# Head attention operands kept head by head: strided writes on VectorE become strided reads on TensorE

## The chip, the cores and the metric

The kernel runs on one core of a Trainium2 chip. The metric is the device time of one execution in microseconds (us), the median of several runs. One more execution was recorded by the hardware profiler; all rows below are from it. Its span is the time from the first to the last recorded instruction.

## What is computed

The input `x` and a context are 32 batches of 256 tokens with 256 features. The reference is, shortened:

```
x = x + tanh(g_xattn) * performer(layernorm(x), ctx, ctx)      # 16 heads, causal, 64 random features
x = x + tanh(g_ffn) * ffn(layernorm(x))
ffn(x):
    h = rmsnorm(x, gamma1)
    q = (h @ Wq + bq).reshape(b, t, 16, 16)
    kv = ((h @ Wdown + bdown) @ Wup + bup).reshape(b, t, 16, 32)
    k, v = split(kv)
    att = softmax(einsum('bthd,btgd->bthg', q, k) / 4)         # heads attend to heads, token by token
    out = einsum('bthg,btgd->bthd', att, v).reshape(b, t, 256)
    x = x + (out @ Wo + bo)
    h2 = rmsnorm(x, gamma2)
    gate = softmax(h2 @ Wg + bg)                               # 8 experts
    return x + einsum('btd,edf,bte->btf', h2, We, gate)
```

The change concerns the attention of heads to heads: for each token a 16 x 16 matrix of scores between its 16 query heads and its 16 key heads, and a mix of the 16 value heads by it. All is float32. Large products are made in three passes of a split into a high and a low part; the scores and the mix are plain float32 matmuls, which the trace shows as two records each.

## The kernel before

All 32 batches go through one software pipeline. Each engine has a fixed order of named steps, a "slot", that is repeated for each batch, with steps of different batches side by side (TensorE makes the scores of batch b while it makes the expert products of batch b-2). A step ends by raising a semaphore, and others wait for that count; `at("q_t", b)` is the end of step `q_t` of batch b. The orders are written out by hand and are the same before and after.

The 256 tokens of a batch lie in two halves of 128 partitions, `qkv[p, t, 768]`. The head attention of a batch goes like this:

- VectorE adds biases (`bqq`, `bkv0`, `bkv1`) into `qkv`, then turns 32 x 32 blocks with one instruction for each of queries, keys and values (`q_t` L1385, `k_t` L1426, `v_t` L1249). Of each block of 32 tokens and 32 values (2 token halves x 16 numbers) it makes one in which the 32 tokens run along the row and the 32 values down the partitions. The results `q_t`, `k_t` and `v_t` hold 32 token positions x 16 heads (or, for `v_t`, 16 numbers of a head) a partition. In the kernel before they are laid out position by position, so a turn writes each next element 16 elements (64 bytes) further.
- ScalarE spreads `q_t` into `q_bd` (two copies, L762) and `k_t` into `k_bd` (four copies, L789), each multiplied by a column of zeros and ones, so that one matmul serves several tokens and keeps them apart. GpSimd does so with `v_t` into `v_bd` (four copies, L475). `v_bd` has a column of ones beside the 16 numbers (`v_one`, L1537, once), from which the sum of the softmax comes.
- TensorE makes the scores (`head_scores`, L1928): for each of the 32 positions n one matmul with 32 columns of `q_bd` as weights and 64 columns of `k_bd` passing through, in four column tiles in turn. VectorE takes the maximum and subtracts it (`s_max`, `s_sub`), ScalarE makes the exponential into `p_bd`, VectorE turns it (`p_t`, L1327).
- TensorE makes the mix (`head_mix`, L1937): for each position a matmul with 32 columns of `p_t` as weights and 68 columns of `v_bd` passing through. VectorE turns the result (`o_tok`, L1362), and GpSimd divides by the sums (`o_n`).

Other steps that the prediction names: `x_raw` (L1322), `c_raw` and `h_raw` (L1391), turns of VectorE with both sides packed; `z` (L1142), the sum over the experts on VectorE, whose last step `a13` releases the store of the batch on the SP queue; the load of the next `x_in` stands behind that store in the SP queue, and also waits for `x1` (`x` L424 in the trace, a GpSimd addition); the statistics of `x_in` on VectorE (`bn`, L1276) wait for that load. In VectorE's slot `v_t` comes right after `a13`, then `h2_lo0`, `h2_lo1`, `ht_lo`, `smax`, and then the statistics. The feature products of the keys on TensorE (L1872) wait for `bqq` (`qkv` L1316), since they use its bank.

Of the kernel before, what the change touches and what calls it, by code (L numbers as in the profile page):

```python
# [7 lines left out]
ALU = mybir.AluOpType  # L8
ACT = mybir.ActivationFunctionType
AX = mybir.AxisListType  # L10

P = 128
NB, L, D = 32, 256, 256
T = L // P
C = D // P
H, HD = 16, 16
# [63 lines left out]
def build(nc, x_d, ctx_d, gx_d, gf_d, rf_d, g1_d, wq_d, bq_d, wdn_d, bdn_d, wup_d, bup_d,  # L80
          wo_d, bo_d, g2_d, wg_d, bg_d, we_d, out_d):
    ctx = ExitStack()
    with ctx:
        def sb(name, shape, dt=F32):
            return ctx.enter_context(nc.sbuf_tensor(name, shape, dt))
# [16 lines left out]
        sel_tok, off_tok, sel_blk = sb("sel_tok", [P, 2]), sb("off_tok", [P, 2]), sb("sel_blk", [P, 4])  # L102
# [33 lines left out]
            stage_f = sb_early("stage_f", [P, P])  # L136

        qkv = sb("qkv", [P, T, 3 * D])
        q_t, k_t, v_t = sb("q_t", [P, 32, H]), sb("k_t", [P, 32, H]), sb("v_t", [P, 32, HD])
        q_bd, v_bd = sb("q_bd", [P, 32, T, H]), sb("v_bd", [P, 32, 4, HD + 1])  # L140
        s_max, s_sub = sb("s_max", [P, 32]), sb("s_sub", [P, 32, H])
        p_bd, p_t = sb("p_bd", [P, 32, T, H]), sb("p_t", [P, 32, 32])

# [35 lines left out]
        nt = sb("nt", [P, QUADS, L])  # L179
        den3 = sb("den3", [P, 3, T, H])  # L180
        o_x = sb("o_x", [P, T, D])
        k_bd = sb("k_bd", [P, 32, 4, H])

        ctx_in, x_load, c_load = transfer("ctx_in", CHUNK_BUFFERS), transfer("x_load", 2), transfer("c_load", 2)
        store = transfer("store", 2)
# [45 lines left out]
        def at(step, b=0):  # L231
            return signal_of[step].at(step, b)

        def up(step, b=0):
            return signal_of[step].up(step, b)
# [125 lines left out]
        def _(pool):  # L361
# [109 lines left out]
            @per_batch  # L471
            def v_bd_(b):
                pool.wait_ge(*at("v_t", b))
                for a in range(4):
                    last = pool.tensor_scalar(v_bd[:, :, a, 0:HD], v_t[:, :, :], sel_blk[:, a:a + 1], 1.0, ALU.mult, ALU.mult)  # L475
                last.then_inc(*up("v_bd", b))

            @per_batch
# [73 lines left out]
            def slot(n):  # L552
                d_v_(n - 4)
                pk2_(n - 2)
                pk3_(n - 2)
                o_n_(n - 5)
                pk0_(n - 2)
                pq0_(n - 2)
                pq1_(n - 2)
                pq2_(n - 2)  # L560
                pq3_(n - 2)
                z0_(n - 5)
                x1_(n - 3)
                r2_(n - 5)
                g_r_(n - 3)
                v1_(n - 2)
                m00_(n - 2)
                m01_(n - 2)
                yb_(n - 4)
                v_bd_(n - 4)  # L570
                q_r_(n - 1)
                k_lo_(n - 1)
                m10_(n - 2)
                m11_(n - 2)
                q_lo_(n - 1)
                pk1_(n - 1)
# [34 lines left out]
        def _(act):  # L611
# [145 lines left out]
            @per_batch  # L757
            def q_bd_(b):
                if b >= 0:
                    act.wait_ge(*at("q_t", b))  # L760
                for t in range(T):
                    act.activation(q_bd[:, :, t, :], q_t[:, :, :], ACT.Copy, scale=sel_tok[:, t:t + 1])  # L762

            @per_batch
            def eq3_(b):
# [18 lines left out]
            @per_batch  # L784
            def k_bd_(b):
                if b >= 0:
                    act.wait_ge(*at("k_t", b))
                for a in range(4):
                    act.activation(k_bd[:, :, a, :], k_t[:, :, :], ACT.Copy, scale=sel_blk[:, a:a + 1])  # L789

            @per_batch
            def x010_(b):
# [64 lines left out]
            def slot(n):  # L857
# [24 lines left out]
                eq1_(n + 4)  # L882
                h_hi_(n + 6)
                q_bd_(n + 2)
                eq3_(n + 4)
                y_(n + 2)
                sq_(n + 1)
                k_bd_(n + 2)
                x010_(n + 4)
                x000_(n + 4)  # L890
# [92 lines left out]
            eq3_(2)  # L983
            we_hi2_()
            q_bd_(0)
            k_bd_(0)
            x000_(2)
            x001_(2)
# [15 lines left out]
            ek1_(3)  # L1004
            ek3_(3)
            q_bd_(1)
            ek0_(3)
            nt1_(2)
# [5 lines left out]
            sq_(0)  # L1014
            y_(1)
            k_bd_(1)
            x000_(3)
            x001_(3)
# [115 lines left out]
        def _(dve):  # L1134
# [111 lines left out]

            @per_batch
            def v_t_(b):
                dve.transpose(v_t[:, :, :].rearrange("p n d -> p d n"), qkv[:, :, 2 * D:3 * D].rearrange("p t (d g) -> p d t g", d=HD)).then_inc(*up("v_t", b))  # L1249

            @per_batch
            def h2_lo0_(b):
# [128 lines left out]
            @per_batch  # L1381
            def q_t_(b):
                if b >= 0:
                    dve.wait_ge(*at("bqq", b))
                dve.transpose(q_t[:, :, :].rearrange("p n h -> p h n"), qkv[:, :, 0:D].rearrange("p t (h d) -> p h t d", d=HD)).then_inc(*up("q_t", b))  # L1385

            @per_batch
            def h_tr_(b):
# [34 lines left out]
            @per_batch  # L1423
            def k_t_(b):
                dve.wait_ge(*at("bkv0", b))
                dve.transpose(k_t[:, :, :].rearrange("p n g -> p g n"), qkv[:, :, D:2 * D].rearrange("p t (g d) -> p g t d", d=HD)).then_inc(*up("k_t", b))  # L1426

            @per_batch
            def a11_(b):
# [104 lines left out]
                rest(wq_lo, stage_q, wq_hi, gamma1).then_inc(*up("wq_lo"))  # L1534

            def v_one_():
                dve.tensor_copy(v_bd[:, :, :, HD], sel_blk[:, :].unsqueeze(1).to_broadcast([P, 32, 4]))  # L1537

            def wdn_lo_():
                rest(wdn_lo, stage_d, wdn_hi, gamma1).then_inc(*up("wdn_lo"))  # L1540
# [27 lines left out]
            def slot(n):  # L1568
# [10 lines left out]
                a03_(n - 1)  # L1579
                a13_(n - 1)  # L1580
                v_t_(n + 1)
                h2_lo0_(n)
                h2_lo1_(n)
# [16 lines left out]
                a1g_(n)  # L1600
                a0g_(n)
                q_t_(n + 2)
                h_tr_(n + 5)
                a10_(n)
# [77 lines left out]
            wdn_lo_()  # L1682
            bqq_(0)
            q_t_(0)
            d_lo_(0)
            h_tr_(3)
# [5 lines left out]
            den_(1)  # L1692
            o_x_(1)
            v_t_(0)
            k_t_(0)
            g_bn_(1)
# [16 lines left out]
            wg_lo_()  # L1713
            p_t_(0)
            q_t_(1)
            o_tok_(0)
            s_rec_(0)
# [7 lines left out]
            g_bn_(2)  # L1725
            y01_(3)
            v_t_(1)
            y00_(3)
            q_bn_(4)
# [117 lines left out]
        def _(pe):  # L1847
# [77 lines left out]
            def head_scores(bank):  # L1925
                for n in range(32):
                    c, m = n % 4, n // 4
                    last = pe.matmul(ps[32 * c:32 * c + 32, bank, :].rearrange("p (a m g) -> p m a g", a=4, m=8)[:, m],  # L1928
                                     q_bd[:, n, :, :].rearrange("p t h -> p (t h)"), k_bd[:, n, :, :],
                                     start=True, stop=True, tile_position=(0, 32 * c))  # L1930
                return last

            def head_mix(banks):
                width = 4 * (HD + 1)
                for n in range(32):
                    a, m = n % 4, n // 4
                    last = pe.matmul(ps[32 * a:32 * a + 32, banks[m // 4], m % 4 * width:(m % 4 + 1) * width],  # L1937
                                     p_t[:, 8 * a + m, :], v_bd[:, 8 * a + m, :, :].rearrange("p c d -> p (c d)"),
                                     start=True, stop=True, tile_position=(0, 32 * a))
                return last  # L1940

# [342 lines left out]
```

## Time and profile before

| | |
|---|---|
| time, median of 3 runs | 1117.84 us (1117.04 to 1120.37) |
| the profiled execution | 1119.66 us |
| its span | 1117.9 us |
| granted TensorE clock, mean | 0.991 of full |
| busy: TensorE matmul / VectorE | 1034.7 / 938.5 us |
| busy: ScalarE / GpSimd | 757.0 / 756.8 us |

Busy time is the time in which an engine had an instruction under way. Matmuls are pipelined, so a busy TensorE is not yet one at its peak; how near it is must be read from what it waits for. `PEld` is TensorE's weight loader, which works beside the matmuls. The first 110 us or so are start-up: loads, a pass over the whole context, splitting of the weights, and the filling of the pipeline.

### The profile page before, as it was taken

What the parts mean: (1) busy time and instruction counts of PE and PEld (TensorE: products, weight loads), DVE (VectorE), ACT (ScalarE), POOL (GpSimd) and SP (SyncE); (2) the same over time, 40 slices, a digit from 0 to 9 for tenths busy, and PEclk for the clock granted to TensorE, in tenths of its full rate; (3) what the DMA queues carried; (4) which work ended last, traced back from release to release, by engine and by line L of the source; (5) the groups of instructions that cost most, each with busy time, mean ns of one, the idle gap of its engine ahead of it and who ended that gap; (6) DMA issues with size and microseconds to landing.
All of it is one profiled execution on the core that took longest, in us unless ns stands there. A gap on an engine that the chain in (4) does not pass through costs nothing.

```text
span 1117.9 us, 31579 instructions
## 1 busy us (share of the span) xinstructions
PE 1034.7 (93%) x12867; PEld 841.2 (75%) x12867; DVE 938.5 (84%) x2173; ACT 757.0 (68%) x1563; POOL 756.8 (68%) x1111
## 2 busy tenths in 40 slices
PE   0576899999999999999999999999999999999988
PEld 0355677778888888778888787888778888888776
DVE  7578678888888988888888888888888988888886
ACT  6666767667776776777677667776776677767531
POOL 3467776677767767777777667776767777777431
PEclk9988899999999999999999999999999999999999
DMA  9410000100001001010010101000000000000000
GB/s 307 142 29 11 21 30 1 30 30 30 30 30 29 11 21 30 30 30 30 30 31 2 29 30 30 30 30 30 24 8 31 29 31 30 30 30 12 11 11 19
DMA packets 38911, 38.63 MB, mean 35 GB/s; under 512 B 3440, under 2 KB 38512, under 8 KB 38768
## 3 DMA queue, kind: packets, MB, share of 16 engines
q1 hardware_dynamic: 38384, 36.59, 10.5%
q8 instruction: 102, 1.67, 0.6%
q14 instruction: 41, 0.34, 0.1%
q0 software_dynamic: 384, 0.04, 0.0%
HBM read 28.23 MB, written 8.39 MB: 33 GB/s over the span
## 4 chain that ended last, share of the span: by engine, by line
PE 52%; DVE 24%; DMA 7%; ACT 7%; POOL 6%; issue 2%; SPq 1%; POOLq 0%; DVEq 0%; ACTq 0%
PE ps L1857 10%; PE ps L1858 7%; PE ps L1859 7%; DVE z L1142 6%; PE ps L1888 6%; PE ps L1903 5%; PE ps L1872 4%; DMA c_in<-in_ctx 4%; DMA x_in<-in_x 3%; PE ps L1937 3%; PE ps L1896 3%; POOL x L424 2%; POOL z L417 2%; DVE k_t L1426 2%; PE ps L1851 2%
## 5 line engine op out<-in xcount | busy, mean ns | idle before, releaser
L1142 DVE SCALAR_TENSOR_TENSOR z<-ps,gate,z 128x256 f32<-128x256 f32 x512 | 234.5, 470 | 17.4 <-PE ps L1859 8.9
L1857 PE MATMUL ps<-we_hi,h_hi 128*128 128x512 f32 (+2 forms) x640 | 238.8, 373 | 5.8 <-DVE s_sub L1296 1.7
L1858 PE MATMUL ps<-we_lo,h_hi 128*128 128x512 f32 (+2 forms) x640 | 223.7, 350 | 0.0
L1859 PE MATMUL ps<-we_hi,h_lo 128*128 128x512 f32 (+2 forms) x640 | 223.7, 349 | 0.0
L1857 PEld LDWEIGHTS ps<-we_hi,h_hi 128*128 128x128 f32 x640 | 120.2, 188 | 44.3 <-issue 18.5
L1888 PE MATMUL ps<-qf,kf 64*128 64x256 f32 x1024 | 137.4, 397 | 11.7 <-POOL qf L408 9.4
L1859 PEld LDWEIGHTS ps<-we_hi,h_lo 128*128 128x128 f32 x640 | 120.2, 188 | 17.2
L1858 PEld LDWEIGHTS ps<-we_lo,h_hi 128*128 128x128 f32 x640 | 120.5, 188 | 11.6
L1888 PEld LDWEIGHTS ps<-qf,kf 64*128 64x128 f32 x1024 | 95.1, 191 | 36.9 <-issue 19.1
L1903 PE MATMUL ps<-att,v 128*32 128x256 f32 (+1 forms) x2048 | 112.4, 339 | 1.2 <-DVE att L1218 0.9
L475 POOL TENSOR_SCALAR v_bd<-v_t,sel_blk 128x512 f32<-128x512 f32 x128 | 88.3, 710 | 13.2 <-DVE v_t L1249 13.2
L1903 PEld LDWEIGHTS ps<-att,v 128*32 128x32 f32 x2048 | 59.3, 112 | 34.4 <-DVE z L1142 4.7
L789 ACT ACTIVATE k_bd<-k_t,sel_blk 128x512 f32<-128x512 f32 x128 | 81.5, 708 | 4.6 <-DVE k_t L1426 4.6
L1896 PEld LDWEIGHTS ps<-qf,kf 64*128 64x128 f32 x1024 | 66.8, 189 | 5.7 <-DVE ht_lo L1265 0.5
L1896 PE MATMUL ps<-qf,kf 64*128 64x128 f32 x1024 | 68.8, 273 | 0.1
L773 ACT ACTIVATE y<-x,shift_f,r_f 128x256 f32<-128x256 f32 x64 | 35.0, 594 | 49.5 <-DVE y L1155 49.5
L397 POOL TENSOR_SCALAR qf<-qf 128x512 f32<-128x512 f32 x32 | 19.9, 621 | 62.9 <-ACT qf L745 62.6
L507 POOL TENSOR_TENSOR q_lo<-x_raw,q_hi 128x512 fp32r<-128x512 f32 x32 | 41.2, 1288 | 30.4 <-ACT q_hi L689 30.4
L415 POOL TENSOR_SCALAR z<-y,tanh_f 128x512 f32<-128x512 f32 x32 | 22.1, 692 | 52.5 <-DVE y L1155 52.5
L643 ACT ACTIVATE nt<-ps 128x512 f32<-128x512 f32 x32 | 19.1, 596 | 55.9 <-PE ps L1903 55.9
L380 POOL TENSOR_TENSOR o_n<-o_tok,s_rec 128x512 f32<-128x512 f32 x32 | 41.6, 1301 | 22.2 <-DVE s_rec L1367 21.8
L739 ACT ACTIVATE ot_hi<-ps 128x512 fp32r<-128x512 f32 x32 | 19.2, 600 | 54.5 <-PE ps L1851 54.4
(218 smaller groups left out, 3077.9 us busy)
## 6 DMA issues: line engine op xcount, KB each, us to landing
x_in<-in_x SPq DMA_DIRECT2D x32, 256.0 KB, 3.3
c_in<-in_ctx SPq DMA_DIRECT2D x32, 256.0 KB, 3.7
out<-z SPq DMA_DIRECT2D x32, 256.0 KB, 2.2
c_chunk<-in_ctx SPq DMA_DIRECT2D x14, 512.0 KB, 8.9
stage<-in_L_ffn_We SPq DMA_DIRECT2D x2, 1024.0 KB, 9.6
c_chunk<-in_ctx SPq DMA_DIRECT2D x2, 256.0 KB, 8.5
stage_u<-in_L_ffn_Wup SPq DMA_DIRECT2D x2, 128.0 KB, 5.7
stage_b<-in_L_ffn_bup SPq DMA_DIRECT2D x1, 256.0 KB, 6.1
```

Source lines behind the costliest of these rows:

```text
L380: pool.tensor_tensor(o_n[:, :, :].rearrange("p t (h d) -> p d t h", d=HD), o_tok[:, 0:HD, :, :], s_rec[:, :, :].unsqueeze(1).to_broadcast( ...
L475: last = pool.tensor_scalar(v_bd[:, :, a, 0:HD], v_t[:, :, :], sel_blk[:, a:a + 1], 1.0, ALU.mult, ALU.mult)
L507: pool.tensor_tensor(q_lo[:, :], x_raw[:, :], q_hi[:, :].bitcast(F32), ALU.subtract).then_inc(*up("q_lo", b))
L789: act.activation(k_bd[:, :, a, :], k_t[:, :, :], ACT.Copy, scale=sel_blk[:, a:a + 1])
L1142: return dve.scalar_tensor_tensor(out=z[b % 2][:, t, :], in0=ps[:, bank, offset:offset + D], scalar=gate[:, t, ex:ex + 1], in1=z[b % 2][:, ...
L1857: pe.matmul(out, a_hi(c), b_hi(c), start=(c == 0), stop=False)
L1858: pe.matmul(out, a_hi(c), b_lo(c), start=False, stop=False)
L1859: last = pe.matmul(out, a_lo(c), b_hi(c), start=False, stop=(c == C - 1))
L1872: last = pe.matmul(ps[:, BANK[f"f{of}{j}"], :], weight[own, :], src[own, :], start=(n == 0), stop=(n == 2 and not more), tile_position=(32 ...
L1888: last = pe.matmul(ps[:, banks[half], j * L:(j + 1) * L], kf[r, pr, 0:P], qf[r, pr, :], start=True, stop=True)
L1896: last = pe.matmul(ps[:, banks[half], j * P:(j + 1) * P], kf[r, pr, P:L], qf[r, pr, P:L], start=True, stop=True)
L1903: last = pe.matmul(ps[32 * j:32 * j + 32, bank, half * L + part * P:half * L + L], v1[:, part, 8 * oct + 2 * j + half, :], att[:, half, j, ...
```

## The change

The turned tiles and the spread tiles are laid out with the position last: `q_t[p, head, position]` instead of `q_t[p, position, head]`, and likewise `k_t`, `v_t`, `q_bd`, `k_bd` and `v_bd`. A turn then writes packed, and the spreads read and write packed. What is contiguous for a matmul before (all columns of one position) is taken with a step of 32 elements (128 bytes) after: the weights from `q_bd`, the passing columns from `k_bd` and `v_bd`. `p_bd`, `p_t`, `s_sub` and `o_tok` are as before. Sizes, values, counts of instructions, orders and waits are the same.

```
-        q_t, k_t, v_t = sb("q_t", [P, 32, H]), sb("k_t", [P, 32, H]), sb("v_t", [P, 32, HD])
-        q_bd, v_bd = sb("q_bd", [P, 32, T, H]), sb("v_bd", [P, 32, 4, HD + 1])
+        q_t, k_t, v_t = sb("q_t", [P, H, 32]), sb("k_t", [P, H, 32]), sb("v_t", [P, HD, 32])
+        q_bd, v_bd = sb("q_bd", [P, T, H, 32]), sb("v_bd", [P, 4, HD + 1, 32])
-        k_bd = sb("k_bd", [P, 32, 4, H])
+        k_bd = sb("k_bd", [P, 4, H, 32])
     v_bd_ (GpSimd)
-                    last = pool.tensor_scalar(v_bd[:, :, a, 0:HD], v_t[:, :, :], sel_blk[:, a:a + 1], 1.0, ALU.mult, ALU.mult)
+                    last = pool.tensor_scalar(v_bd[:, a, 0:HD, :], v_t[:, :, :], sel_blk[:, a:a + 1], 1.0, ALU.mult, ALU.mult)
     q_bd_, k_bd_ (ScalarE)
-                    act.activation(q_bd[:, :, t, :], q_t[:, :, :], ACT.Copy, scale=sel_tok[:, t:t + 1])
+                    act.activation(q_bd[:, t, :, :], q_t[:, :, :], ACT.Copy, scale=sel_tok[:, t:t + 1])
-                    act.activation(k_bd[:, :, a, :], k_t[:, :, :], ACT.Copy, scale=sel_blk[:, a:a + 1])
+                    act.activation(k_bd[:, a, :, :], k_t[:, :, :], ACT.Copy, scale=sel_blk[:, a:a + 1])
     v_t_, q_t_, k_t_ (VectorE)
-                dve.transpose(v_t[:, :, :].rearrange("p n d -> p d n"), qkv[:, :, 2 * D:3 * D].rearrange("p t (d g) -> p d t g", d=HD)).then_inc(*up("v_t", b))
+                dve.transpose(v_t[:, :, :], qkv[:, :, 2 * D:3 * D].rearrange("p t (d g) -> p d t g", d=HD)).then_inc(*up("v_t", b))
-                dve.transpose(q_t[:, :, :].rearrange("p n h -> p h n"), qkv[:, :, 0:D].rearrange("p t (h d) -> p h t d", d=HD)).then_inc(*up("q_t", b))
+                dve.transpose(q_t[:, :, :], qkv[:, :, 0:D].rearrange("p t (h d) -> p h t d", d=HD)).then_inc(*up("q_t", b))
-                dve.transpose(k_t[:, :, :].rearrange("p n g -> p g n"), qkv[:, :, D:2 * D].rearrange("p t (g d) -> p g t d", d=HD)).then_inc(*up("k_t", b))
+                dve.transpose(k_t[:, :, :], qkv[:, :, D:2 * D].rearrange("p t (g d) -> p g t d", d=HD)).then_inc(*up("k_t", b))
     v_one_ (VectorE, once)
-                dve.tensor_copy(v_bd[:, :, :, HD], sel_blk[:, :].unsqueeze(1).to_broadcast([P, 32, 4]))
+                dve.tensor_copy(v_bd[:, :, HD, :], sel_blk[:, :].unsqueeze(2).to_broadcast([P, 4, 32]))
     head_scores, head_mix (TensorE)
-                                     q_bd[:, n, :, :].rearrange("p t h -> p (t h)"), k_bd[:, n, :, :],
+                                     q_bd[:, :, :, n].rearrange("p t h -> p (t h)"), k_bd[:, :, :, n],
-                                     p_t[:, 8 * a + m, :], v_bd[:, 8 * a + m, :, :].rearrange("p c d -> p (c d)"),
+                                     p_t[:, 8 * a + m, :], v_bd[:, :, :, 8 * a + m],
```

## Rows read from the trace of the kernel before

**Rows 1.** The page: busy time of each engine, share of the span.

```profile
PE 1034.7 (93%) x12867; PEld 841.2 (75%) x12867; DVE 938.5 (84%) x2173; ACT 757.0 (68%) x1563; POOL 756.8 (68%) x1111
```

**Rows 2.** Windows of 200 us: length, busy us of each engine, clock, DMA.

```profile
600.00:800.00 200.00, 197.66 (x2457) 161.90 (x2455) 173.88 (x413) 141.97 (x299) 142.90 (x209) 1.00 0.08 26
```

**Rows 3.** The chain, 550 to 640 us: start us, us, what (two scores, one mix).

```profile
551.27 0.89 PE ps L1928 x64
...
583.16 0.89 PE ps L1928 x64
...
593.46 1.03 PE ps L1937 x64
```

**Rows 4.** Waits of TensorE and its loader, 200 to 1000 us: total us, times, longest.

```profile
PE ps L1872 <- DVE qkv L1316: 5.6, 10, 0.7
...
PEld ps L1872 <- DVE qkv L1316: 8.9, 14, 0.9
PEld ps L1857 <- ACT qf L730: 5.9, 25, 0.2
PEld ps L1903 <- DVE z L1142: 4.2, 25, 0.2
PEld ps L1937 <- DVE down L1332: 4.1, 17, 0.3
```

**Rows 5.** The chain again, 600 to 635 us, three of its pieces.

```profile
602.44 1.08 DVE k_t L1426
...
614.84 5.03 DMA c_in<-in_ctx
...
629.66 1.08 DVE q_t L1385
```

**Rows 6.** Waits of VectorE, 200 to 1000 us.

```profile
DVE bn L1276 <- DMA x_in<-in_x: 28.0, 25, 2.1
DVE bn6g L1198 <- POOL x L424: 24.2, 25, 1.1
```

**Rows 7.** Groups by line and form: VectorE's turns; busy us, mean ns, idle before.

```profile
L1426 DVE STREAM_TRANSPOSE k_t<-qkv 128x512 f32<-128x512 f32 x32 | 35.1, 1098 | 1.0
L1385 DVE STREAM_TRANSPOSE q_t<-qkv 128x512 f32<-128x512 f32 x32 | 34.2, 1070 | 0.0
L1249 DVE STREAM_TRANSPOSE v_t<-qkv 128x512 f32<-128x512 f32 x32 | 33.8, 1057 | 0.0
...
L1362 DVE STREAM_TRANSPOSE o_tok<-ps 128x544 f32<-128x544 f32 x32 | 23.6, 739 | 1.9 <-PE ps L1937 1.9
...
L1322 DVE STREAM_TRANSPOSE x_raw<-xn 128x512 f32<-128x512 f32 x32 | 22.3, 697 | 0.7 <-ACT xn L670 0.6
```

**Rows 8.** Line L1519 in the start-up: ns min/median/max of two instructions.

```profile
L1519 DVE TENSOR_TENSOR wup_lo<-stage_u,wup_hi x2: 416/710/1003, 61.8 to 62.1; 128x256 fp32r<-128x256 f32 x2
```

**Rows 9.** Timeline of VectorE: start us, us, what.

```profile
629.66 1.08 DVE L1385 STREAM_TRANSPOSE q_t<-qkv 128x512 f32<-128x512 f32 x1
630.57 0.70 DVE L1391 STREAM_TRANSPOSE h_raw<-h2e 128x512 f32<-128x512 f32 x1
631.17 0.99 DVE L1142 SCALAR_TENSOR_TENSOR z<-ps,gate,z 128x256 f32<-128x256 f32 x2
```

**Rows 10.** Groups by line and form: spreads and their nearest packed likes.

```profile
L475 POOL TENSOR_SCALAR v_bd<-v_t,sel_blk 128x512 f32<-128x512 f32 x128 | 88.3, 710 | 13.2 <-DVE v_t L1249 13.2
L789 ACT ACTIVATE k_bd<-k_t,sel_blk 128x512 f32<-128x512 f32 x128 | 81.5, 708 | 4.6 <-DVE k_t L1426 4.6
...
L805 ACT ACTIVATE h2n<-y,r 128x256 f32<-128x256 f32 x64 | 28.8, 501 | 2.8 <-POOL r L431 2.8
...
L415 POOL TENSOR_SCALAR z<-y,tanh_f 128x512 f32<-128x512 f32 x32 | 22.1, 692 | 52.5 <-DVE y L1155 52.5
```

**Rows 11.** Groups by line and form: the mix and score matmuls, 32 batches.

```profile
L1937 PE MATMUL ps<-v_bd,p_t 128*32 128x68 f32 x2048 | 36.9, 224 | 4.7 <-POOL down_v L365 2.1 <-DVE p_t L1327 1.5 <-DVE down L1332 0.6
...
L1928 PE MATMUL ps<-k_bd,q_bd 128*32 128x64 f32 x2048 | 36.2, 225 | 0.0
```

## The prediction

> **What bounds the kernel now.** I read the page first. TensorE is busy for 93% of the span, VectorE for 84%, the other two for 68% [rows 1]. The windows view says more, because it leaves the start out: between 600 and 800 us TensorE is busy 197.7 of 200 us at the full clock, VectorE 173.9 [rows 2]. The reader is to see that a batch of the steady part has almost no time in which TensorE has nothing in hand. One batch takes 31.9 us: the same stage, the 64 small score matmuls, starts at 551.27 and at 583.16 us [rows 3].
>
> The waits view of TensorE shows how close it is to its own bound. Over 25 batches (200 to 1000 us) it and its weight loader waited 5.6 + 8.9 us for the bias addition on `qkv`, 5.9 us for ScalarE's exponential, 4.2 us for the last `z` and 4.1 us for `down` [rows 4]. That is 28.7 us, or 1.15 us in each batch of 31.9. So TensorE's own work would need about 30.75 us a batch, and 1.15 us is all that a quicker VectorE or ScalarE could give it.
>
> The chain that ended last shows the second loop. It does not stay on TensorE: through the batch after 600 us it runs over VectorE's `k_t` turn, GpSimd's `z` and `x1`, the last `z` of the batch before, the store and load on SP, the `c_in` transfer (5.03 us), and back over `q_t` to the next `k_t` [rows 5]. This loop takes the same 31.9 us. Two loops of equal length hold each other: shortening one alone brings little beyond the slack that the other has, lengthening either costs.
>
> VectorE itself waits in each batch for `x_in` to land (28.0 us over 25) and for `x1` (24.2 us) [rows 6].
>
> **The three turns on VectorE.** `k_t`, `q_t` and `v_t` take 1098, 1070 and 1057 ns for 512 elements a partition. `x_raw`, the same operation and size with both sides packed, takes 697 ns [rows 7]. Two things differ: the three read runs of 16, and they write every element 64 bytes after the last. The change leaves the reads and makes the writes packed. Which one costs? `o_tok` reads with a step of 17 elements (from PSUM) and writes packed: 739 ns for 544 elements, the packed rate. And in the start-up two `wup_lo` subtractions of equal size take 416 and 1003 ns; the slower is the half whose elements are written (and `wup_hi` read) 64 bytes apart [rows 8] (GpSimd was at work beside it, so its size is not clean). I put the cost on the written step. Since neighbours on VectorE overlap a little, I take start-to-start times: `q_t` to the next 0.91 us, the packed `h_raw` to the next 0.60 us [rows 9]. Saving 0.31 us a turn, 0.93 us a batch; bounds are nothing (if the reads are to blame) and 1098 + 1070 + 1057 - 3 x 697 = 1.13 us.
>
> Not all of it counts. `v_t` stands between the last `z` of a batch, which releases the store and the next `x_in` load, and the batch statistics that wait for this `x_in`; VectorE waits there 1.1 us in every batch [rows 6], so 0.31 us saved in `v_t` becomes 0.31 us more of waiting. `q_t` and `k_t` lie on the second loop [rows 5]: 0.62 us a batch is what that loop becomes shorter.
>
> **ScalarE and GpSimd.** The spreads write the same 512 elements, from packed to packed instead of in runs of 16. `k_bd` takes 708 ns; the scaled copy `h2n` of 256 elements, packed, takes 501, and both are (708 - 501)/256 = 0.81 ns an element: no cost of the runs is to be seen, so I take nothing. The far bound is an unscaled 512-element copy at about 0.6 us, 0.1 us less for each of six. `v_bd` takes 710 ns against 692 for the packed `z` product [rows 10]: 4 x 0.018 = 0.07 us a batch. Both engines are idle for 32% of the span [rows 1], and that covers it. `v_one` runs once.
>
> **The matmuls.** Here the change adds. A batch has 64 score matmuls of 64 columns and 64 mix matmuls of 68 [rows 11]: 32 products, two records each, spread over four column tiles that run side by side. The scores take 0.89 us: 16 records follow one another in a tile, so a column takes 0.89/(16 x 64) = 0.87 ns. The mix takes 1.03 us, 0.95 ns a column [rows 3]. In this form each column comes from the address next to the last. After the change each comes 128 bytes further, in `k_bd` and `v_bd`, and so do the 32 columns of each `q_bd` weight load. No row shows TensorE reading like that. Bounds: nothing, if a stream that asks for a column every 0.87 ns gets it from anywhere. From the other side, the nearest row is VectorE's stream in steps of 64 bytes, an element in 0.91/512 = 1.78 ns [rows 9]. If TensorE's four streams each fall to that pace, a column costs 0.91 ns more in the scores and 0.83 in the mix: 16 x 64 x 0.91 = 0.93 us and 16 x 68 x 0.83 = 0.90 us, 1.83 us a batch. The outer bound is that the four streams then also take turns: 64 x 64 x 0.87 = 3.56 us instead of 0.89, 64 x 68 x 0.87 = 3.79 instead of 1.03, 5.43 us a batch. I take 1.83. It is a stream to SBUF that I compare with a stream from it, of another engine: that is the weakest link of this prediction.
>
> The Trainium skill (Advanced Engine Details and Errata, Memory Cachelines) speaks against the change at this place: SBUF has lines of 16 bytes, and a stream needs at least two hits in a line or it pays. Packed float32 has four hits a line, a step of 128 bytes has one. The page says nothing of its size or of TensorE in particular; by it the sum has some cost above nothing. The turns on VectorE agree with it, 1070 against 697 ns [rows 7]; for TensorE nothing here shows it.
>
> The strided weight loads of `q_bd` have 32 columns each; at 0.9 ns more a column a load grows by 29 ns, and it lies behind a matmul of its own tile that then takes 64 x 1.78 = 114 ns. Taken at nothing; if that cover fails, see the rivals.
>
> **The sum.** TensorE: 30.75 + 1.83 = 32.6 us of own work. The second loop: 31.9 - 0.62 = 31.3, now 1.3 us shorter than TensorE's, so most of TensorE's waits go: each is a wait for something that the added 0.9 us in front of it lets arrive. The score results are used by `s_max`, behind which VectorE waits for `x_in` anyway [rows 6], so their lateness goes no further. I let 0.25 us of the 1.15 us of waits stay: 32.85 us a batch, 0.95 more than 31.9. Times 32 batches is 30.4 us. On the profiled execution (span 1117.9, whole time 1119.66) this gives a span of 1148 and a time of 1150; the median of the runs shown is 1.8 us lower than that execution, so **1148 us**. With all waits gone it is 0.7 x 32 = 22 us (1140), with none gone 1.83 x 32 = 59 (1177). The likeliest case's own range is 1133 to 1180.
>
> **The rivals.**
> *TensorE reads the step for nothing (chance 0.25).* For it: its float32 columns come at only 0.87 ns, slowly for a stream. Then VectorE's 0.62 us a batch count, within TensorE's slack of 1.15: -0.62 x 32 = -20 us, 1098 us. It decides up to an added cost of about 0.9 us a batch (what TensorE's waits absorb), that is 0.9/2112 = 0.43 ns for each of the 16 x 132 = 2112 columns a batch: under 1.3 ns a column the kernel is not slower.
> *The four streams share one path (0.18).* Against it: today four run at 0.87 ns a column each without slowing each other. For it: a shared path may be just wide enough for packed columns. 5.43 - 0.9 = 4.53 us a batch, +145: 1263 us, and TensorE the only bound.
> *The weight loads are what grows (0.07).* The 64 loads of the scores start 13.9 ns apart; if they are made one after another and a load then takes 32 x 1.78 = 57 ns, the scores take 3.65 us, +2.76, with the 0.90 of the mix 3.66, less 0.9: 2.76 x 32 = +88, 1206 us.
> *The turns do not get faster, since the runs of 16 that they read are what costs (0.05).* Then the second loop stays 31.9, TensorE's waits go only in part: about +1.3 x 32 = 42, 1160 us.
>
> **The numbers.** The forecast has 0.45. A measurement of this kernel tells a difference of 0.3% (3.4 us) from none. Faster by more holds most of the free rival: 0.22. Within 0.3% lies the narrow strip where the added cost is near 0.9 us a batch: 0.06. Slower: 0.72. The range has to hold cases of both signs: from 1096, just below the free rival, up to 1245, which leaves out most of the shared path and little else.
>
> **What the profile after would show.** The three turns at about 0.7 us. The score stage at 1.8 us and the mix at 1.9 instead of 0.89 and 1.03 in the chain. The waits for `qkv` and `down` on TensorE nearly gone, its busy share above 99%. VectorE's wait for `x_in` in each batch no shorter. `k_bd`, `q_bd` and `v_bd` unchanged within 0.02 us. The prediction is wrong if the score stage keeps 0.9 us (then 1098) or takes over 3 us (then above 1200), or if the stages grow as said and TensorE keeps its waits.

## The result

The changed kernel takes 1187.6 us (median of 5 runs, 1185.84 to 1189.66) against 1117.5 us (median of 5 runs of the kernel before; three of them gave the 1117.84 above): the ratio is 1.062 (95% interval 1.060 to 1.064), 70 us slower. The forecast was 1148 us with a range of 1096 to 1245: the right side and inside the range, but 30 us of a loss of 70. The profiled execution took 1185.84 us, with a span of 1184.1.

### The profile after

The page, busy time of each engine and the chain by engine, answers to [rows 1]:

```profile
PE 1112.0 (94%) x12867; PEld 928.1 (78%) x12867; DVE 919.4 (78%) x2173; ACT 755.9 (64%) x1563; POOL 758.4 (64%) x1111
...
PE 87%; DVE 4%; ACT 4%; POOL 2%; DMA 1%; issue 1%; SPq 0%; DVEq 0%; POOLq 0%; ACTq 0%
```

VectorE has less to do than before, and the chain now runs over TensorE for 87% of the span; before it was 52%, with VectorE at 24%. The window of [rows 2] after the change:

```profile
600.00:800.00 200.00, 199.81 (x2375) 167.54 (x2378) 159.25 (x388) 133.05 (x281) 137.36 (x200) 1.00 0.08 25
```

TensorE is busy in 199.8 of 200 us, at the full clock as before. The groups by line and form: turns, matmuls and weight loads, to be held against [rows 7] and [rows 11].

```profile
L1928 PE MATMUL ps<-k_bd,q_bd 128*32 128x64 f32 x2048 | 90.8, 358 | 0.0
...
L1928 PEld LDWEIGHTS ps<-k_bd,q_bd 128*32 128x32 f32 x2048 | 82.8, 158 | 0.3 <-issue 0.3
...
L1937 PE MATMUL ps<-v_bd,p_t 128*32 128x68 f32 x2048 | 66.5, 295 | 3.8 <-POOL down_v L365 2.1 <-DVE p_t L1327 1.1 <-DVE down L1332 0.5
...
L1426 DVE STREAM_TRANSPOSE k_t<-qkv 128x512 f32<-128x512 f32 x32 | 22.7, 710 | 1.0
L1385 DVE STREAM_TRANSPOSE q_t<-qkv 128x512 f32<-128x512 f32 x32 | 22.4, 700 | 0.0
L1249 DVE STREAM_TRANSPOSE v_t<-qkv 128x512 f32<-128x512 f32 x32 | 22.4, 699 | 0.0
```

The turns are at 0.70 us as forecast. A mix record went from 224 to 295 ns, a score record from 225 to 358: the two stages read with the same step and do not pay the same. How long a stage is shows best from its first start to the start of the group behind it. The timeline of TensorE after, start us, us (the last end is modelled, so a group's own length is longer than the way to the next start; the 1.03 us of the mix in [rows 3] has such an end), what:

```profile
611.29 2.83 PE L1928 MATMUL ps<-k_bd,q_bd 128*32 128x64 f32 x64
613.79 0.98 PE L1903 MATMUL ps<-att,v 128*32 128x256 f32 x16
...
623.41 2.08 PE L1937 MATMUL ps<-v_bd,p_t 128*32 128x68 f32 x64
625.28 0.86 PE L1903 MATMUL ps<-att,v 128*32 128x256 f32 x16
```

The same view before:

```profile
582.98 1.08 PE L1928 MATMUL ps<-k_bd,q_bd 128*32 128x64 f32 x64
583.87 0.83 PE L1903 MATMUL ps<-att,v 128*32 128x256 f32 x16
...
593.34 1.16 PE L1937 MATMUL ps<-v_bd,p_t 128*32 128x68 f32 x64
594.28 0.86 PE L1903 MATMUL ps<-att,v 128*32 128x256 f32 x16
```

The scores went from 0.89 to 2.50 us, the mix from 0.94 to 1.87 us. The first group behind the scores also starts slower, by 0.15 us (0.91 instead of 0.76 us to the next). Together 1.61 + 0.15 + 0.93 = 2.69 us a batch on TensorE, where the forecast had 1.83.

I took such stage starts from the timelines of all batches between 200 and 1000 us and averaged the distances. One batch: 32.10 us before, 34.37 after, so 2.27 us more; TensorE gave back 2.69 - 2.27 = 0.42 us of waiting. The same starts give a check that needs no wait: the shortest batches before take 31.72 us, and 31.72 + 2.69 = 34.41 us is what a batch takes after, to 0.04 us. The waits view of the weight loader after answers to [rows 4]:

```profile
PEld ps L1857 <- ACT qf L730: 5.4, 23, 0.2
PEld ps L1903 <- DVE z L1142: 3.9, 23, 0.2
```

The waits for `qkv` and `down` are gone. Those for ScalarE and for `z` are as they were in each batch (0.2 us), although a batch is 2.3 us longer. And VectorE, against [rows 6]:

```profile
DVE s_max L1270 <- PE ps L1928: 45.4, 24, 2.0
DVE z L1142 <- PE ps L1859: 22.1, 26, 1.0
...
DVE qkv L1316 <- PE ps L1859: 18.4, 24, 0.9
...
DVE bn L1276 <- DMA x_in<-in_x: 0.5, 2, 0.3
```

It no longer waits for `x_in` (28.0 before, 0.5 after): it waits for the scores instead (45.4), right before. The prediction had expected this wait for `x_in` to stay as it was.

### The profile page after: what moved, and what is told of

Its sections match the earlier page's. It is cut to its first block, busy times and chain, and to the rows that moved or that the text cites. A ratio compares the mean times of both kernels' runs of the same rounds, so it can differ in the third digit from the quotient of the medians.

```text
span 1184.1 us, 31579 instructions
## 1 busy us (share of the span) xinstructions
PE 1112.0 (94%) x12867; PEld 928.1 (78%) x12867; DVE 919.4 (78%) x2173; ACT 755.9 (64%) x1563; POOL 758.4 (64%) x1111
## 4 chain that ended last, share of the span: by engine, by line
PE 87%; DVE 4%; ACT 4%; POOL 2%; DMA 1%; issue 1%; SPq 0%; DVEq 0%; POOLq 0%; ACTq 0%
PE ps L1857 15%; PE ps L1859 12%; PE ps L1858 12%; PE ps L1888 10%; PE ps L1903 7%; PE ps L1928 7%; PE ps L1937 5%; PE ps L1896 5%; PE ps L1872 5%; PE ps L1851 2%; PE ps L1913 2%; PE ps L1921 1%; PE ps L1922 1%; DMA c_chunk<-in_ctx 1%; ACT k_bd L789 1%
## 5 line engine op out<-in xcount | busy, mean ns | idle before, releaser
L1142 DVE SCALAR_TENSOR_TENSOR z<-ps,gate,z 128x256 f32<-128x256 f32 x512 | 235.7, 472 | 43.2 <-PE ps L1859 31.7
L1903 PEld LDWEIGHTS ps<-att,v 128*32 128x32 f32 x2048 | 69.7, 115 | 31.6 <-DVE z L1142 4.7
L1928 PE MATMUL ps<-k_bd,q_bd 128*32 128x64 f32 x2048 | 90.8, 358 | 0.0
L1928 PEld LDWEIGHTS ps<-k_bd,q_bd 128*32 128x32 f32 x2048 | 82.8, 158 | 0.3 <-issue 0.3
L1937 PE MATMUL ps<-v_bd,p_t 128*32 128x68 f32 x2048 | 66.5, 295 | 3.8 <-POOL down_v L365 2.1
L489 POOL TENSOR_TENSOR k_lo<-c_raw,k_hi 128x512 fp32r<-128x512 f32 x32 | 41.5, 1298 | 40.8 <-ACT k_hi L664 40.7
L1270 DVE TENSOR_REDUCE s_max<-ps 128x32 f32<-128x512 f32 x32 | 22.1, 692 | 57.9 <-PE ps L1928 57.9
L1937 PEld LDWEIGHTS ps<-v_bd,p_t 128*32 128x32 f32 x2048 | 58.4, 124 | 8.1 <-issue 2.9
```

The lines of the kernel that those rows point to most:

```text
L1142: return dve.scalar_tensor_tensor(out=z[b % 2][:, t, :], in0=ps[:, bank, offset:offset + D], scalar=gate[:, t, ex:ex + 1], in1=z[b % 2][:, ...
L1903: last = pe.matmul(ps[32 * j:32 * j + 32, bank, half * L + part * P:half * L + L], v1[:, part, 8 * oct + 2 * j + half, :], att[:, half, j, ...
```

## The experiments

All times are medians; those of the kernel before, run beside them, were 1117.5 (with the first four kernels below `after`), 1117.4 (steps 2 and 4, swapped positions, one tile after the other), 1119.5 (both kernels with spreads that take a step, and the other order) and 1117.7 us (the last). "Scores" and "mix" are stage lengths from start to next start, medians of the batches between 200 and 1000 us; "one batch" is the mean there.

| kernel | scores | mix | one batch | time | ratio, interval |
|---|---|---|---|---|---|
| before | 0.89 | 0.94 | 32.10 | 1117.5 | |
| after | 2.50 | 1.87 | 34.37 | 1187.6 | 1.062 (1.060 to 1.064) |
| keys and values | 2.66 | 1.87 | 34.44 | 1189.7 | 1.064 (1.061 to 1.068) |
| queries only | 1.33 | 0.94 | 32.37 | 1124.1 | 1.006 (1.004 to 1.008) |
| values only | 0.89 | 1.87 | 33.02 | 1146.1 | 1.025 (1.022 to 1.029) |
| keys only | 2.65 | 0.94 | 33.53 | 1163.4 | 1.0405 (1.037 to 1.044) |
| keys and values, positions swapped | 1.77 | 2.71 | 34.52 | 1190.9 | one run |
| keys only, one tile after the other | 5.3 | 2.9 | 38.70 | 1326.4 | one run |
| step 2 | 0.96 | 1.01 | 32.13 | 1116.7 | 0.9987 (0.9974 to 1.0000) |
| step 4 | 1.91 | 1.98 | 33.80 | 1169.4 | 1.046 (1.044 to 1.048) |
| turns packed, spreads write with a step | 0.89 | 0.94 | 33.14 | 1150.0 | 1.028 (1.025 to 1.030) |
| turns packed, spreads read with a step | 0.89 | 0.94 | 33.66 | 1169.1 | 1.045 (1.042 to 1.048) |
| after, scores issued in another order | 1.79 | 1.88 | 33.55 | 1162.4 | 1.039 (1.036 to 1.043) |
| step 2 for queries and keys only | 0.97 | 0.94 | 32.05 | 1114.7 | 0.9969 (0.9954 to 0.9985) |

The scores vary from batch to batch where they are long or their weight loads have a step: 2.50 to 2.70 us in `after`, 2.53 to 2.68 with keys and values, 1.31 to 1.39 with the queries only. Each of the two kernels whose spreads take a step has one long batch near 200 us (37.6 and 38.3 us); without it their means are 32.95 and 33.45.

### Parts of the change

Four kernels have only some of the tiles head by head. For the keys the edit is

```
-        k_bd = sb("k_bd", [P, 32, 4, H])
+        k_bd = sb("k_bd", [P, 4, H, 32])
-                    act.activation(k_bd[:, :, a, :], k_t[:, :, :], ACT.Copy, scale=sel_blk[:, a:a + 1])
+                    act.activation(k_bd[:, a, :, :], k_t[:, :, :], ACT.Copy, scale=sel_blk[:, a:a + 1])
-                dve.transpose(k_t[:, :, :].rearrange("p n g -> p g n"), ...
+                dve.transpose(k_t[:, :, :], ...
-                                     q_bd[:, n, :, :].rearrange("p t h -> p (t h)"), k_bd[:, n, :, :],
+                                     q_bd[:, n, :, :].rearrange("p t h -> p (t h)"), k_bd[:, :, :, n],
```

and the lines of the change's own diff for the queries and for the values.

Keys and values:

> Keys and values head by head as in the changed kernel, queries (q_t, q_bd) as before: the passing columns of scores and mix come with a step of 32, the weight loads are packed. Theory 1, the strided weight loads are what makes the score stage 0.8 us longer than forecast (2.50 instead of about 1.8 us): scores 1.8 us, mix 1.87 us. Rival, the score stage's passing columns alone cost that much (a score matmul writes runs of 16 in PSUM, the mix one run of 68): scores stay at 2.5 us. For the time: the changed kernel gained 70 us for 2.7 us of added TensorE time a batch, 26 us for each; if that holds here, 1.86 us gives +48, 1166 us. If TensorE's waits absorb 0.9 us a batch as the prediction had it, about 1148 us.

The timeline:

```profile
578.55 2.93 PE L1928 MATMUL ps<-k_bd,q_bd 128*32 128x64 f32 x64
581.21 0.92 PE L1903 MATMUL ps<-att,v 128*32 128x256 f32 x16
```

The scores took 2.66 us with packed weight loads, more than the 2.50 with strided ones (why more is open). Theory 1 fell: the weight loads are not what makes the scores longer than forecast. Both expected times, 1166 and 1148 us, were too low as well: 1189.7.

Queries only:

> Only the queries head by head: 64 weight loads of 32 columns a batch come with a step of 32, all passing columns are packed. Theory 1a, a strided load is slower whatever passes: 57 ns or so instead of 27, and as it does not hide behind a matmul of 56 ns the score stage grows by 0.5 to 0.8 us, to 1.4 to 1.7 us; time about 1117 + 0.8 x 26 = 1138, less what the shorter q_t gives. Theory 1b, a strided load hides behind packed columns and costs only where the passing columns are strided too: score stage 0.9 to 1.0 us, and the time 1110 to 1118, because q_t is 0.31 us shorter.

The timeline shows the strided weight loads alone:

```profile
587.17 1.58 PE L1928 MATMUL ps<-k_bd,q_bd 128*32 128x64 f32 x64
588.56 0.84 PE L1903 MATMUL ps<-att,v 128*32 128x256 f32 x16
```

1.39 us here and 1.33 as the median, 0.44 to 0.50 more: at the lower end of theory 1a. With packed columns a strided load does not hide; in the changed kernel, whose columns are slower, it adds nothing to be seen. The time rose by 6.6 us (1138 less something was expected) and a batch by 0.27 us, less than the stage.

Values only:

> Only the values head by head: mix 1.87 us instead of 0.94, scores 0.89 as before, v_t 0.70 us. If TensorE's waits of before (1.15 us a batch by the waits view) absorb up to 0.9 us, the time stays within 1115 to 1123 us. If nearly none of them is time that could be filled, +0.93 us a batch at 26 us each: 1141 us. The wait for x_in takes up what v_t saves in either case.

Keys only:

> Only the keys head by head: scores 1.8 us instead of 0.89, mix as before. Absorbing theory: the shorter k_t (0.31 us on the second loop) and the waits cover it, 1112 to 1120 us. Rival: +0.93 us a batch at 26 us each, 1141 us. Together with the values alone it should give the time of keys and values together, if TensorE is the only bound.

Here is the second error. The values add 0.93 us a batch to TensorE and a batch grows by 0.92: nothing is absorbed, and the time is 1146 instead of 1115 to 1123. The keys add about 1.8 us (the stage, 2.6 and not the 1.8 expected, and the start of the group behind) and a batch grows by 1.43: 0.4 us is absorbed. The two losses, 28.6 and 45.9 us, add up to 74.5 us, against 72.2 for keys and values together. The timeline of the kernel before tells where the slack lies. The key features behind the scores that start at 582.98 (above), and the scores and key features of the next batch:

```profile
590.54 0.50 PE L1872 MATMUL ps<-k_hi,f_hi 32*128 32x512 f32 x4
...
614.71 1.08 PE L1928 MATMUL ps<-k_bd,q_bd 128*32 128x64 f32 x64
...
623.03 0.51 PE L1872 MATMUL ps<-k_hi,f_hi 32*128 32x512 f32 x4 [0.71 <-DVE qkv L1316]
```

The distances are 7.56 and 8.32 us. Over 24 batches it is 7.84 us on average and 7.54 at least: some 0.3 us a batch is a wait that can be filled, not the 14.5/25 = 0.58 that the waits view gives. The next distance, to the mix, is 2.88 us on average against 2.81 to 2.82 with the keys, with both and after: 0.07 us. Together this is 0.4 us, not 1.15, and it is also what lies between the mean batch and the shortest one, 32.10 - 31.72. The shortest batch plus the stages' growth gives the batches of other kernels too: with the values 31.72 + 0.93 = 32.65 us (the shortest there is 32.64, the mean 33.02), with the keys 31.72 + 1.83 = 33.55 (33.48, 33.53), with a step of 4 31.72 + 2.06 = 33.78 (33.76, 33.80). With the values alone the 0.4 us stay unfilled. Both lie between the scores and the mix, so growth in the scores uses them. Growth in the mix comes behind, and VectorE waits for the mix itself. Its waits with the values alone:

```profile
DVE bn L1276 <- DMA x_in<-in_x: 30.8, 25, 2.3
...
DVE z L1142 <- PE ps L1859: 16.5, 25, 0.7
...
DVE o_tok L1362 <- PE ps L1937: 3.9, 7, 0.9
```

`z` waited 2.5 us for TensorE over the same stretch before and waits 16.5 now. I read it so: the lateness goes to the last `z`, from there to `x_in` and to the `qkv` that TensorE waits for, and its wait stays (the distance is 7.83 us on average, as before). The two loops of the prediction are then one, as VectorE's part hangs on TensorE's products. The waits fit this; no run cuts the path.

### Why the scores pay more than the mix

Both read with a step of 128 bytes. But the scores give neighbouring positions to the four column tiles that run side by side, the mix gives them positions 8 apart. The next kernel swaps this. Its products go where they went but come from other positions, so its output is not the attention; sizes and counts are the same.

```
-                                     q_bd[:, n, :, :].rearrange("p t h -> p (t h)"), k_bd[:, :, :, n],
+                                     q_bd[:, 8 * c + m, :, :].rearrange("p t h -> p (t h)"), k_bd[:, :, :, 8 * c + m],
-                                     p_t[:, 8 * a + m, :], v_bd[:, :, :, 8 * a + m],
+                                     p_t[:, n, :], v_bd[:, :, :, n],
```

> Keys and values head by head as in the run with both, but the positions are taken in the other order: the four column tiles of the scores, which run side by side, read positions 8 apart (32 bytes), those of the mix read neighbouring positions (4 bytes apart). The products are those of permuted positions. Theory: what makes a strided score column cost 2.5 ns and a strided mix column 1.7 ns is that in the scores the four tiles read at nearly the same addresses. Then the stages change places: scores 64/68 of 1.87 us, about 1.75 us, mix about 2.7 us. Rival: it is the output (the scores write runs of 16, the mix one run of 68) or the stage itself: scores stay at 2.6 us, mix at 1.87 us.

The timeline of TensorE:

```profile
579.24 1.97 PE L1928 MATMUL ps<-k_bd,q_bd 128*32 128x64 f32 x64
581.00 0.85 PE L1903 MATMUL ps<-att,v 128*32 128x256 f32 x16
...
590.47 3.09 PE L1937 MATMUL ps<-v_bd,p_t 128*32 128x68 f32 x64
593.33 0.89 PE L1903 MATMUL ps<-att,v 128*32 128x256 f32 x16
```

Scores 1.76 us, mix 2.86 us (1.77 and 2.71 as medians): the stages changed places, as the theory says, and the rival, the way in which the output is written, fell, since that did not change. The other half of the argument leaves each product where it was and changes only the order of issue in the changed kernel, so that no two of the four tiles are less than 5 positions apart (each is 9 from its neighbour in the issue, but for the wrap at 8):

```
-                for n in range(32):
+                for n in (4 * ((m + 2 * c) % 8) + c for m in range(8) for c in range(4)):
```

> The changed kernel with the 32 score products issued in another order only: the four tiles that run side by side take positions 9 or more apart instead of neighbours, each into the place in PSUM that it had. Theory (neighbouring positions read at once are what makes a strided score column cost 2.5 ns instead of 1.7): scores 1.8 to 2.0 us instead of 2.50, 0.5 to 0.7 us less a batch, all of it on TensorE: 1167 to 1173 us instead of 1187.6. If the strided weight loads then show (0.5 us in the run with the queries alone), scores 2.3 us and 1181 us. If nothing comes of the order: 1187 us.

The timeline:

```profile
599.72 1.98 PE L1928 MATMUL ps<-k_bd,q_bd 128*32 128x64 f32 x64
601.51 0.84 PE L1903 MATMUL ps<-att,v 128*32 128x256 f32 x16
```

This order also changes which places of the output are written side by side; in the swapped kernel they stayed as they were, so the reading is what both have in common. The scores take 1.79 us instead of 2.50, and the kernel 1162.4 instead of 1187.6 us: 25 us come back for one line, a little more than the 15 to 21 expected. At 1.79 us the stage pays 0.88 ns more than packed for each of the 1024 columns that pass through one tile in a batch, about the size that the prediction had for it (0.91), and the strided loads cost almost nothing beside them (1.79 us against 1.77 with packed ones).

Is the cost one of each stream or of the four together? One kernel (keys head by head) goes through the positions of one tile before the next, in both stages:

```
-                for n in range(32):
+                for n in (4 * m + c for c in range(4) for m in range(8)):
```

> Keys alone head by head; and both stages go through the eight positions of one column tile before the next tile, so that the matmuls no longer run side by side in four tiles. The mix then shows a lone packed stream, the scores a lone strided one. If a strided stream is limited by itself (each column goes to another place and takes about 1.7 ns however many tiles run), a score record takes 64 x 1.7 = 110 ns or more against 60 to 80 for a packed mix record: 64 records 7 us against 4 to 5 us. If the limit is one that the four streams share, a lone strided stream runs at the packed pace and the scores take no longer than 64/68 of the mix.

The timeline, lone strided columns in the scores, lone packed ones in the mix:

```profile
600.57 5.56 PE L1928 MATMUL ps<-k_bd,q_bd 128*32 128x64 f32 x61
...
605.96 0.40 PE L1928 MATMUL ps<-k_bd,q_bd 128*32 128x64 f32 x2
...
615.76 3.15 PE L1937 MATMUL ps<-v_bd,p_t 128*32 128x68 f32 x61
...
618.74 0.34 PE L1937 MATMUL ps<-v_bd,p_t 128*32 128x68 f32 x3
```

61 score records take 605.96 - 600.57 = 5.39 us, 88 ns each or 1.38 ns a column; 61 mix records take 2.98 us, 49 ns each or 0.72 ns a column (a weight load that does not hide would be in both). A lone stream pays for the step by itself, about twofold. With four side by side a column of a tile takes 0.87 ns packed, 1.72 with a step and 8 positions apart, and 2.4 to 2.6 with a step and neighbouring. So part of the price is each stream's own, and a second part comes only when tiles that run side by side read neighbouring addresses. The one run took 1326.4 us, since the tiles' overlap was given up.

### How long a step may be

`S` neighbouring positions stand innermost in all six tiles:

```
+        q_t, k_t, v_t = sb("q_t", [P, G, H, S]), sb("k_t", [P, G, H, S]), sb("v_t", [P, G, HD, S])
+        q_bd, v_bd = sb("q_bd", [P, G, T, H, S]), sb("v_bd", [P, G, 4, HD + 1, S])
+        k_bd = sb("k_bd", [P, G, 4, H, S])
+                                     q_bd[:, n // S, :, :, n % S].rearrange("p t h -> p (t h)"), k_bd[:, n // S, :, :, n % S],
```

with G = 32/S, and the turns, spreads and the mix to match. The step is then S elements, and a turn writes runs of S.

> All six tiles laid out with pairs of neighbouring positions innermost: the matmuls read with a step of 2 elements (8 bytes), the turns write runs of 2. By the 16-byte lines of the Trainium skill (Advanced Engine Details and Errata, Memory Cachelines) two reads still fall into one line, so that scores and mix stay at 0.9 us; a cost that comes with any step would give 1.8 and 2.5 us. The turns lie between 0.70 and 1.07 us; if runs of 2 are enough for the writes, 0.70 us, and q_t and k_t bring the second loop down by 0.6 us a batch: 1100 us. If neither changes, 1117 us.

> As the step of 2, with four neighbouring positions innermost: a step of 4 elements (16 bytes). Every column then is in a line of its own, as with the step of 32. Theory of lines: scores 2.5 us and mix 1.87 us as in the changed kernel, and its time, about 1187 us. [...] The turns write runs of 4 (16 bytes): 0.70 us.

The timelines of the scores, step 2 and then step 4 (in these kernels the lines stand one further down):

```profile
585.02 1.16 PE L1929 MATMUL ps<-k_bd,q_bd 128*32 128x64 f32 x64
585.99 0.84 PE L1904 MATMUL ps<-att,v 128*32 128x256 f32 x16
...
604.63 2.10 PE L1929 MATMUL ps<-k_bd,q_bd 128*32 128x64 f32 x64
606.54 0.85 PE L1904 MATMUL ps<-att,v 128*32 128x256 f32 x16
```

With a step of 2 the stages are 0.96 and 1.01 us, 0.07 more than packed each; with a step of 4, 1.91 and 1.98. The large price comes between 8 and 16 bytes. That is where the lines of the Trainium skill (Advanced Engine Details and Errata, Memory Cachelines) have it, two reads in a line of 16 bytes, and TensorE's times fit the rule, but for the 7 to 8% that 8 bytes cost. The distance beyond a line is not what costs: the mix takes 1.98 us at 16 bytes and 1.87 at 128. The scores with a step of 4 did not take the 2.5 us expected, though their four tiles read neighbours as well, and the time was 1169.4 us and not 1187. Neighbours cost more only at the wide step, and why is open.

The turns took 0.70 us with runs of 2 already, and yet the time did not move. The waits of VectorE with a step of 2 say why:

```profile
DVE bn L1277 <- DMA x_in<-in_x: 29.3, 25, 2.2
...
DVE z L1143 <- PE ps L1860: 10.6, 27, 0.9
...
DVE s_max L1271 <- PE ps L1929: 5.3, 24, 0.2
```

`z` waits 10.6 us for TensorE instead of 2.5 and `s_max` 5.3: some 13 us over 25 batches of the 23 that the turns gave back went into waiting for products. A batch stayed at 32.13 us and the time at 1116.7, where the second loop would have given 1100.

### The turns without TensorE's part

> The VectorE part of the change alone: the three turns write packed (head by head), and the spreads of ScalarE and GpSimd bring the numbers back into position order by writing with a step, so that every matmul reads packed as before. Turns 0.70 us, scores 0.89, mix 0.94. As the prediction had it (q_t and k_t on a second loop that is as long as TensorE's): 0.62 us a batch, 1098 us. As the run with a step of 2 suggests (the turns were 0.7 us there and nothing came of it, VectorE only waited more for TensorE): 1112 to 1118 us. If strided writes cost ScalarE and GpSimd as much as VectorE (0.3 us or more each, ten a batch), later than that: above 1121 us.

> As the run before, but the spreads read with a step and write in runs of 16. Turns, scores and mix the same. The question is only which side of a spread bears a step better: k_bd and q_bd at 0.71 and 0.72 us, v_bd at 0.70 us if a step costs these engines nothing, about 1 us and more if it costs them what it costs VectorE. Time as in the run before if both are free.

The turns write packed, TensorE reads packed, and the spreads do the reordering:

```
-                    act.activation(k_bd[:, :, a, :], k_t[:, :, :], ...
+                    act.activation(k_bd[:, :, a, :].rearrange("p n g -> p g n"), k_t[:, :, :], ...
```

(in the second kernel the `rearrange` stands on `k_t`). Groups by form, spreads writing with a step:

```profile
L475 POOL TENSOR_SCALAR v_bd<-v_t,sel_blk 128x512 f32<-128x512 f32 x128 | 144.8, 1228 | 13.8 <-DVE v_t L1249 13.8
L789 ACT ACTIVATE k_bd<-k_t,sel_blk 128x512 f32<-128x512 f32 x128 | 129.4, 1162 | 3.5 <-DVE k_t L1426 3.5
```

1.23 and 1.16 us instead of 0.71 [rows 10]; reading with a step costs as much, 1.18 and 1.19. `q_bd` takes 1.25 and 1.26 us instead of 0.72. Ten spreads a batch pay where three turns gained, and the last expectation, above 1121 us, is the one that held: 1150 and 1169 us. The waits of TensorE tell the place (spreads writing with a step):

```profile
PEld ps L1857 <- DVE z L1142: 23.7, 23, 1.1
...
PE ps L1857 <- ACT att L794: 22.7, 24, 2.8
```

ScalarE's copies of `att` stand behind the four `k_bd`, and TensorE waits for them; before, this wait came in one batch of 25 (0.9 us).

### A version that is a little faster

Queries and keys with a step of 2, values as before:

> Queries and keys with a step of 2 as in that run, values position by position as in the kernel before. v_t is 1.06 us again, the mix 0.94 us. The step of 2 cost 0.05 us a batch in the mix and gave 0.31 us in v_t; if v_t's saving is worth nothing (VectorE waits for x_in behind it) the time is that of the run with a step of 2 for all, or 1 to 2 us lower: 1112 to 1117 us. If v_t's saving counted there, 1120 us or more.

1114.7 us, ratio 0.9969 (0.9954 to 0.9985), and a batch of 32.05 us: 3 us below the kernel before and the fastest seen. `v_t` back at 1.06 us cost nothing. The 2 us against the step of 2 for all tiles are what the packed mix accounts for, 0.07 us in each of 32 batches. That is what is left of the idea: the layout that keeps two neighbours together is packed enough for VectorE and nearly so for TensorE.

## Why the prediction was off

By its own steps:

- **The three turns**: right. 0.70 us each, and it is the written step that had cost (runs of 2 written are enough, the reads never changed).
- **`v_t` worth nothing**: right; the last kernel gives the saving up and loses nothing. **`q_t` and `k_t` worth 0.62 us a batch**: wrong. The step-2 kernel has them both and stays at 32.13 us; the last kernel, with the mix packed too, gains 0.05 and pays 0.07 in the scores, so they are worth about 0.12. The chain's second loop was taken for a loop of its own; the waits show its `z` waiting for TensorE's products as soon as VectorE is early. In the forecast this term only served to let TensorE's waits go.
- **ScalarE and GpSimd unchanged**: right for this change (`k_bd` 0.71 us, `v_bd` 0.72).
- **The mix**: forecast +0.90, measured +0.93 us. The forecast's start of 1.03 us has the modelled end in it; with 0.94 us, 0.86 ns a column, the same sum would have given 1.00.
- **The scores**: forecast +0.93 us, measured +1.61, and 0.15 in the group behind. This is the term that failed most. The prediction compared the stream with VectorE's turn, and the sizes agree (1.72 and 1.78 ns). That is luck as far as the runs show: they give no reason why two engines should pay alike, and a lone stream of TensorE takes 1.38 ns. And the prediction let the four tiles run free of each other; in the scores they read neighbouring addresses, and then a column takes 2.4 to 2.6 ns. The rival of a shared path had a true part in it, but it put the scores at 3.56 us and the mix at 3.79, where 2.50 and 1.87 were measured. The failed term is 1.61 + 0.15 - 0.93 = 0.83 us a batch on TensorE, some 25 us of the time: the reordered issue gave 25 us back.
- **The waits that TensorE gives back**: forecast 0.9 us a batch, measured 0.42; the missing 0.48 us are some 15 us of the time. The 1.15 us read from the waits view is not all time that can be filled, and TensorE's own work was not 30.75 us a batch but 31.7. The waits of 0.2 us for ScalarE and `z` stand in every batch, before and after, with about the same length; what can be filled is the spread of the distances between stages, 0.3 and 0.07 us. And the mix alone fills none of it.
- **The signs in the profile**: the turns, the mix at 1.9 us, the gone waits for `qkv` and `down`, TensorE busy above 99% and the unchanged spreads came as said. The score stage and the wait for `x_in` did not: that wait turned into one for the scores, whose lateness the prediction had let end there.

The sum with measured terms: 2.69 - 0.42 = 2.27 us for a batch in the middle, where the forecast had 0.95. Over all 32 the profiled spans differ by 66.2 us, 2.07 a batch; the two batches that start at about 163 and 197 us, with 33.6 us each before, grow by 1.6 and 1.5 us only.

The forecast's rival of a free step is ruled out: TensorE pays about twofold for steps of 16 and of 128 bytes, and 7 to 8% more for one of 8.

## What to carry to other kernels

Before moving a strided access to TensorE to spare VectorE, count how often each side passes over it: here scattered float32 numbers cost three turns 0.31 us each, and TensorE, which reads the spread copies in two records for each product, 2.7 us a batch. If a layout must serve a turn and a matmul, keep two float32 neighbours together; the turns then ran at the packed pace and the matmuls within 7 to 8% of it. Where matmuls in several column tiles read with a wide step, let the tiles that run side by side read far apart. And before counting on an engine's listed waits as slack, look at how much the distance between its stages varies from batch to batch: the shortest batch shows what the engine needs.

## What the runs showed of the hardware

- Float32 columns read by TensorE: alone 0.72 ns packed and 1.38 ns with a step of 128 bytes; four tiles side by side 0.87 ns a column in each packed, 1.72 with the step, 2.4 to 2.6 with the step and neighbouring addresses.
- With a step of 8 bytes the two stages took 7 to 8% longer, with one of 16 bytes about twice as long.
- 64 weight loads of 32 columns with a step of 128 bytes added 0.44 to 0.50 us beside packed columns and nothing to be seen beside strided ones (2.50 us with, 2.66 without; in the other order of issue 1.79 with, and 1.77 without in the swapped kernel).
- ScalarE and GpSimd paid 0.45 to 0.55 us when one side of a 512-element copy went through float32 numbers 128 bytes or more apart, on the read and the write side alike; VectorE's turn paid 0.31 us from start to start (0.37 us of its own length) for writing them 64 bytes apart.
